# A graph kernel's adjacency: scratch as 512-byte rows, transposed flat in four pieces of 125 columns

## The chip, the cores and the metric

The program runs on one core of a Trainium2 chip. The metric is the device time of one execution in microseconds.

## The reference

A batch of 2048 samples, each with 50 nodes of 32 features, and two maskers. What matters here is how the adjacency is made and used:

```
adj = einsum('bn,tnm->btm', x.reshape(b, 1600), masker_param) + masker_bias
adj = relu(adj).reshape(b, 2, 50, 50)
adj = adj / (adj.sum(axis=-1, keepdims=True) + 1e-6)
m = einsum('btnd,de->btne', h, weight); m = einsum('btnm,btmd->btnd', adj, m)
gates = m @ w_ih.T + b_ih + h @ w_hh.T + b_hh
h = (1 - z) * tanh(r * ng) + z * h        # r, z, ng from gates
```

After that `h` is normalised over the batch and over each sample, scored, and pooled with a softmax. The inputs and outputs are float32; the first stage multiplies in split float32r parts.

## The kernel before, in words

The samples are in 16 tiles of 128. Three stages run one after the other, each with its own block of instructions per engine; semaphores order the engines, and each engine's order is written out by hand.

**First stage** (`stage1`). For each of two blocks of 8 tiles it goes through 10 groups of 500 adjacency columns (`GN` = 10 nodes n by 50 nodes m). A group and a tile make a *window*, 160 in all. PE (`window`, L344) accumulates 38 products of 128x128 by 128x500 into a bank. ACT (`relu`, L227) evacuates it, DVE (`normalise`, L278 to L286) sums the rows and multiplies by the reciprocal, PE (`transposes`, L324) turns the result, ACT (`evacuate`, L233) copies it to `at`, and SP (`store_tile`, L136) stores it to the scratch tensor `adjT` in device memory. PE does the transposes of a window in the middle of the products of the next one, after the fourth pair of chunks (`T_AT`). `u`, `an`, `at` and the banks have two buffers each. DVE writes `an` as 5 pairs of nodes, each node padded from 50 to 64 columns, so that a transpose of 128 columns puts node q on partitions 0 to 49 and node q + 5 on partitions 64 to 113. The pad is zeroed once at the start (L272).

`adjT` is laid out [tile, sample half, m, node, 64 samples]; a row of a store is 5 nodes x 64 samples, 1280 bytes, and there are two stores of 100 rows for each window.

**Second stage** (`stage2`). It works in rounds: 8 rounds of 4 samples per quarter tile make one tile, and two tiles (r = 0, 1, one buffer each) make an iteration. In each round PE aggregates (`aggregate`, L679: the tile's adjacency `adj_sb` times `xs_sb`), ACT and DVE split the result, PE computes the gates (L704, L710), ACT applies the sigmoids and the tanh (L524, L529, L534), DVE updates `h` (L585 to L600). PE turns the chunks of the tile before (L721), ACT copies them to `hC` (L502) and stores them from its own DMA queue (`store`, L509, seven per tile).

SP loads for each tile the adjacency (`load_adj`, L443, one DMA of 100 rows x 25.6 KB into partitions (sample half, m)) and the features `xs_sb` (L445, two DMAs). It issues them for tile t + 2 when PE has aggregated the last round of tile t (`ax_done`); PE waits for them (`adj_loaded`) one round ahead of their first use, at the seventh round of tile t + 1. ACT loads `xg_sb`, the features in another layout, for tile t + 1 in the first round of tile t (`load_xg`, L481), and casts it in four parts (`x_hi`, L490), of which the first stands in the fourth round, in ACT's order ahead of that round's sigmoids. Queue q1 of the profile is SP's, q10 is ACT's.

**Third stage** (`stage3`) reads `h` back (L854, in 512-byte pieces) and pools; it does not touch the adjacency.

Of the kernel before, what the change touches and what calls it, by code (L numbers as in the profile page):

```python
# [15 lines left out]
fp32 = mybir.dt.float32  # L16
# [5 lines left out]
B, N, D, T = 2048, 50, 32, 2  # L22
TN = T * N
P = 128
# [10 lines left out]
GN = 10  # L35
# [3 lines left out]
BLOCKS = TILES // BLK  # L39
ITERS = BLOCKS * GROUPS  # L40
MPAD = 64
SH = P // 2
PAIRS = GN // 2
EPS_ROW = 1e-6
EPS = 1e-5

# [34 lines left out]
def stage1(nc, psum, xT, W, adjT, ident_d):  # L81
    with ExitStack() as ctx:
# [7 lines left out]
        w_raw = sb("w_raw", [P, KC + 1, GW])  # L90
        ident = sb("ident_sb", [P, P])
        u = sb("u", [P, 2, GN, N])
        an = sb("an", [P, 2, PAIRS, 2, MPAD])
        rows = sb("rows", [P, 3, GN])
        at = sb("at", [P, 2, 2, PAIRS, SH])

        x_loaded, ident_loaded = [sem("x_loaded0"), sem("x_loaded1")], sem("ident_loaded")
        w_loaded = [sem(f"w_loaded{i}") for i in range(NU)]
# [2 lines left out]
        mm_done, u_ready, an_ready = sem("mm_done"), sem("u_ready"), sem("an_ready")  # L101
        tr_done, at_ready = sem("tr_done"), sem("at_ready")
        at_stored = [sem("at_stored0"), sem("at_stored1")]
        pad_zeroed, dve_step = sem("pad_zeroed"), sem("dve_step")

        def mm_out(c2):

# [1 line left out]

        def tr_out(c2):  # L110

            return psum[:, (2 + 2 * c2) * BANK:(2 + 2 * c2) * BANK + PAIRS * P]

        block = ctx.enter_context(nc.Block())

        @block.sync
        def _(sp):
            def load_x(bt, half):

                if bt >= 1:  # L120
                    sp.wait_ge(x_ready, 2 * bt - 1 + half)
                k0, k1 = XHALVES[half]
                sp.dma_start(x_raw[:, k0:k1, :], xT[bt, :, k0:k1, :]).then_inc(x_loaded[half], 16)

            def load_w(i, group, after):

                if after is not None:
                    sp.wait_ge(w_ready, after)
                sp.dma_start(w_raw[:, 2 * i:2 * i + 2, :], W[group, i] if isinstance(group, int) else
                             W[bass.ds(group, 1), i].rearrange("g p k n -> p (g k) n")).then_inc(w_loaded[i], 16)  # L130

            def store_tile(c, c2, tile, group):

                sp.wait_ge(at_ready, c + 1)
                for half in range(2):
                    sp.dma_start(adjT[tile, :, :, bass.ds(group * GN + half * PAIRS, PAIRS), :].rearrange("h m c s -> m h c s"),  # L136
                                 at[MPAD * half:MPAD * half + N, c2]).then_inc(at_stored[c2], 16)

            load_x(0, 0)
            for i in range(NU):  # L140
                load_w(i, 0, None)
                if i == 0:
                    load_x(0, 1)
            sp.dma_start(ident[:, :], ident_d).then_inc(ident_loaded, 16)
            for blk in range(BLOCKS):
                for it, group in p1_iters(sp, blk):
                    for w in range(BLK):
                        if isinstance(it, int) and it == 0 and w + 1 < BLK:
                            load_x(w + 1, 0)
                            load_x(w + 1, 1)  # L150
                        if not (isinstance(it, int) and it == ITERS - 1):
                            nxt = 0 if isinstance(it, int) and it % GROUPS == GROUPS - 1 else group + 1

                            for i in range(NU):
                                if w == (min(i + 1, BLK - 2) if isinstance(it, int) and it == 0 else 1):
                                    load_w(i, nxt, it * NU + i + 1)
                        c = it * BLK + w
                        if w > 0:
                            store_tile(c - 1, (w - 1) % 2, blk * BLK + w - 1, group)
                        elif not (isinstance(it, int) and it == 0):  # L160
                            if isinstance(it, int) and it % GROUPS == 0:
                                store_tile(c - 1, 1, blk * BLK - 1, GROUPS - 1)
                            else:
                                store_tile(c - 1, 1, blk * BLK + BLK - 1, group - 1)
                        if isinstance(it, int) and it == GROUPS - 1 and blk + 1 < BLOCKS:
                            load_x(BLK + w, 0)
                            load_x(BLK + w, 1)
            store_tile(ITERS * BLK - 1, 1, TILES - 1, GROUPS - 1)
            sp.wait_ge(at_stored[0], 32 * (ITERS * BLK // 2))
            sp.wait_ge(at_stored[1], 32 * (ITERS * BLK // 2))  # L170

        def split_x_hi(act, bt, half):
            act.wait_ge(x_loaded[half], 16 * (bt + 1))
# [48 lines left out]
        def _(act):  # L222
# [6 lines left out]
            def evacuate(c, c2, start=False):  # L229
                act.wait_ge(tr_done, c + 1)  # L230
                if not start:
                    act.wait_ge(at_stored[c2], 16 * (c - c2))
                nc.scalar.copy(at[:, c2].rearrange("p h q s -> p q h s"),  # L233
                               tr_out(c2).rearrange("p (q h s) -> p q h s", q=PAIRS, h=2)).then_inc(at_ready, 1)

            split_x_hi(act, 0, 0)
            for i in range(NU):
# [31 lines left out]

        @block.vector  # L270
        def _(dve):
            nc.vector.memset(an[:].rearrange("p c q h m -> p (c q h m)"), 0.0).then_inc(pad_zeroed, 1)  # L272
            dve.wait_ge(pad_zeroed, 1)

            def normalise(c, c2, start=False):

                dve.wait_ge(u_ready, c + 1)
# [5 lines left out]
                dve.wait_ge(dve_step, 3 * c + 3)  # L283
                if not start:
                    dve.wait_ge(tr_done, c - 1)
                nc.vector.tensor_tensor(an[:, c2, :, :, 0:N].rearrange("p q h m -> p h q m"),  # L286
                                        u[:, c2].rearrange("p (h q) m -> p h q m", h=2),
                                        rows[:, 2].rearrange("p (h q) -> p h q", h=2).unsqueeze(3).to_broadcast([P, 2, PAIRS, N]),
                                        ALU.mult).then_inc(an_ready, 1)

            split_x_lo(dve, 0, 0)
# [26 lines left out]
        def _(pe):  # L318
            def transposes(c, c2, start=False):
                pe.wait_ge(an_ready, c + 1)  # L320
                if not start:
                    pe.wait_ge(at_ready, c - 1)
                for q in range(PAIRS):
                    last = nc.tensor.transpose(tr_out(c2)[:, q * P:(q + 1) * P],  # L324
                                               an[:, c2, q].rearrange("p h m -> p (h m)"), ident[:, :])
                last.then_inc(tr_done, 1)

            def window(it, w, blk, c, start=False, bank_free=False, none_before=False):
# [54 lines left out]
def stage2(nc, psum, ins, adjT, hF, stats):  # L383


    with ExitStack() as ctx:
# [53 lines left out]
        @block.sync  # L440
        def _(sp):
            def load_adj(tile, r):
                sp.dma_start(adj[:, r], adjT[tile].rearrange("h m c s -> (h m) c s")).then_inc(adj_loaded[r], 16)  # L443
                for half in range(2):
                    sp.dma_start(xs[N * half:N * half + N, r, half], ins["xm"][tile, half]).then_inc(adj_loaded[r], 16)  # L445

# [219 lines left out]
        def _(pe):  # L666
# [15 lines left out]
            def gates(it, s, more):  # L682
# [2 lines left out]
                    pe.wait_ge(xg_ready, (it * 2 + r + 1) * XPARTS)  # L685

                if s == ROUNDS - 2:
                    pe.wait_ge(adj_loaded[1], (it + 1) * 48)
                if s == S - 2 and more:
                    pe.wait_ge(adj_loaded[0], (it + 2) * 48)  # L690
                pe.wait_ge(m_ready, it * S + s + 1)
                xb = [t[:, r, q].unsqueeze(1).to_broadcast([P, T, N * QB]) for t in (xg_hi, xg_lo)]
                def terms(of):
# [34 lines left out]
                        aggregate((s + 1) % S)  # L728
                    gates(it, s, more)

            pe.wait_ge(adj_loaded[0], 48)
            aggregate(0)
            pe.wait_ge(ident_loaded, 16)
            turn(0, True)
# [513 lines left out]


def program(nc, ins, out):  # L1250
    adjT = nc.dram_tensor("adjT", [TILES, 2, N, TN, SH], fp32, kind="Internal").ap()
    hF = nc.dram_tensor("hF", [TILES, P, FC, P], fp32, kind="Internal").ap()
    with nc.psum_tensor("psum", [P, 8 * BANK], fp32) as psum:
        stage1(nc, psum, ins["xT"], ins["W"], adjT, ins["ident"])
# [69 lines left out]
```

## Time and profile before

| | |
|---|---|
| median of 3 runs | 2437.35 us (2435.56 to 2440.09) |
| the profiled execution | 2435.1 us |
| its span | 2433.3 us |
| mean granted TensorE clock | 0.966 |
| PE busy | 2279.1 us, 94% |
| DVE, ACT, POOL busy | 1103.7, 975.1, 135.1 us |

A group of rows in the profile is one line of the kernel on one engine; its busy time is the time in which at least one of its instructions ran, so a mean times a count can be more than the busy time where instructions overlap. A wait is put down to what released it last. A DMA share is the mean over the 16 DMA engines, where packets that overlap on one engine count twice.

### The profile page before, as it was taken

To read this page: it belongs to the slowest core of one execution; us is meant where nothing else is said; L and a number is where in the kernel's file an instruction comes from. 1 tells how busy PE (TensorE), PEld (TensorE's weight loads), DVE (VectorE), ACT (ScalarE), POOL (GpSimd) and SP (SyncE) were. 2 spreads that over 40 slices of the span, in tenths; PEclk is the share of its full clock that TensorE was granted. 3 is DMA by queue.
4 is the path that set the end of the run, shared out by engine and by line. 5 is a ranking of instruction groups with operands and counts; after the bars stand their busy time and mean duration, and the time that the engine had idled before them with its cause. 6 is when DMAs were issued, how large, how long until landed. Compare 5 with 4: busy or idle time off the path is not lost. (4 is left out here: it accounts for less than half of the span.)

```text
span 2433.3 us, 35457 instructions
## 1 busy us (share of the span) xinstructions
PE 2279.1 (94%) x12462; PEld 1815.6 (75%) x12462; DVE 1103.7 (45%) x2191; ACT 975.1 (40%) x1625; POOL 135.1 (6%) x124
## 2 busy tenths in 40 slices
PE   8999999999999999999999993999999999957787
PEld 7888888888888888888888882887878777832333
DVE  5333223233244332223333222677778777764456
ACT  4322212222233222122222121777778777746340
POOL 0000000000000000000000000111111101004230
PEclk9999999999999999999999996999999999977899
DMA  6321122221253220222220213445455454338430
GB/s 225 122 84 48 69 84 88 88 84 39 75 178 119 85 89 28 86 88 85 87 86 28 88 29 107 129 141 149 142 146 153 139 152 135 111 105 204 128 93 5
DMA packets 137744, 250.97 MB, mean 103 GB/s; under 512 B 11734, under 2 KB 97398, under 8 KB 134390
## 3 DMA queue, kind: packets, MB, share of 16 engines
q1 hardware_dynamic: 119546, 212.59, 28.5%
q10 hardware_dynamic: 18144, 37.69, 4.8%
q8 instruction: 29, 0.48, 0.1%
q14 instruction: 25, 0.20, 0.0%
HBM read 182.54 MB, written 67.70 MB: 103 GB/s over the span
## 5 line engine op out<-in xcount | busy, mean ns | idle before, releaser
L344 PE MATMUL psum<-w_hi,x_lo 128*128 128x500 f32 x2080 | 821.0, 395 | 8.2 <-DVE w_lo L214 8.2
L344 PE MATMUL psum<-w_lo,x_hi 128*128 128x500 f32 (+1 forms) x2080 | 810.3, 390 | 0.0
L344 PE MATMUL psum<-w_hi,x_hi 128*128 128x500 f32 x1920 | 746.1, 389 | 0.0
L278 DVE TENSOR_REDUCE rows<-u 128x10 f32<-128x500 f32 x160 | 107.6, 673 | 919.3 <-ACT u L227 919.1
L344 PEld LDWEIGHTS psum<-w_hi,x_lo 128*128 128x128 f32 x2080 | 391.6, 188 | 83.7 <-issue 8.2
L344 PEld LDWEIGHTS psum<-w_lo,x_hi 128*128 128x128 f32 (+1 forms) x2080 | 392.2, 189 | 75.3
L344 PEld LDWEIGHTS psum<-w_hi,x_hi 128*128 128x128 f32 x1920 | 360.9, 188 | 73.4
L233 ACT COPY at<-psum 128x640 f32<-128x640 f32 x160 | 111.0, 693 | 699.8 <-PE psum L324 699.8
L679 PE MATMUL psum<-adj_sb,xs_sb 100*64 100x100 f32 x2048 | 239.7, 391 | 29.6 <-DMA xs_sb<-xm 29.6
L679 PEld LDWEIGHTS psum<-adj_sb,xs_sb 100*64 100x64 f32 x2048 | 197.8, 219 | 64.3 <-issue 64.3
L227 ACT ACTIVATE u<-psum 128x500 f32<-128x500 f32 x160 | 94.0, 587 | 334.2 <-PE psum L344 334.2
L657 POOL TENSOR_TENSOR xg_lo<-xg_sb,xg_hi 128x400 fp32r<-128x400 f32 x64 | 66.8, 1046 | 2044.6 <-ACT xg_hi L490 2044.6
L524 ACT ACTIVATE r_gate<-psum,bias 64x400 f32<-64x400 f32 x256 | 151.0, 590 | 57.0 <-PE psum L704 55.3
L214 DVE TENSOR_TENSOR w_lo<-w_raw,w_hi 128x1000 fp32r<-128x1000 f32 x120 | 144.1, 1201 | 25.8 <-ACT w_hi L208 19.8
L208 ACT CAST w_hi<-w_raw 128x1000 fp32r<-128x1000 f32 (+1 forms) x140 | 135.6, 969 | 46.8 <-PE psum L344 45.3
L529 ACT ACTIVATE psum<-psum,bias 64x400 f32<-64x400 f32 x256 | 141.2, 552 | 3.9 <-DVE hG L600 0.5
L608 DVE BATCH_NORM_STATS2 stats<-hC 128x128 f32 (+1 forms) x400 | 88.5, 281 | 68.9 <-ACT hC L502 68.7
L324 PE MATMUL psum<-ident_sb,an 128*128 128x128 f32 x800 | 113.3, 272 | 3.9 <-DVE an L286 3.9
L324 PEld LDWEIGHTS psum<-ident_sb,an 128*128 128x128 f32 x800 | 97.1, 140 | 24.6 <-DVE an L286 3.0
L286 DVE TENSOR_TENSOR an<-u,rows 128x500 f32<-128x500 f32 x160 | 108.8, 680 | 6.9
L585 DVE SCALAR_TENSOR_TENSOR n_in<-psum,bias,r_gate 128x400 f32<-128x400 f32 x128 | 80.3, 627 | 57.3 <-PE psum L710 28.7
L1027 DVE SCALAR_TENSOR_TENSOR pr<-h,nmu_sb,psum 128x512 f32<-128x512 f32 x100 | 71.1, 743 | 52.2 <-PE psum L1187 31.6
(162 smaller groups left out, 2319.6 us busy)
## 6 DMA issues: line engine op xcount, KB each, us to landing
w_raw<-W SPq DMA_DIRECT2D x140, 500.0 KB, 6.8
adjT<-at SPq DMA_DIRECT2D x320, 125.0 KB
adj_sb<-adjT SPq DMA_DIRECT2D x16, 2500.0 KB
hF<-hC ACTq DMA_DIRECT2D x96, 256.0 KB, 2.2
h<-hF SPq DMA_DIRECT2D x64, 256.0 KB, 4.6
xs_sb<-xm SPq DMA_DIRECT2D x32, 400.0 KB
xg_sb<-xg ACTq DMA_DIRECT2D x14, 800.0 KB, 13.4
h<-hF SPq DMA_DIRECT2D x48, 192.0 KB, 3.8
```

The costliest lines, as they stand in the source:

```text
L208: nc.scalar.copy(w_hi[:, k0:k1, :], w_raw[:, k0:k1, :]).then_inc(w_hi_ready, 1)
L214: nc.vector.tensor_tensor(w_lo[:, k0:k1, :], w_raw[:, k0:k1, :], w_hi[:, k0:k1, :].bitcast(fp32), ALU.subtract).then_inc(w_ready, 1)
L227: nc.scalar.activation(u[:, c2].rearrange("p n m -> p (n m)"), mm_out(c2), ACT.Relu).then_inc(u_ready, 1)
L233: nc.scalar.copy(at[:, c2].rearrange("p h q s -> p q h s"), tr_out(c2).rearrange("p (q h s) -> p q h s", q=PAIRS, h=2)).then_inc(at_ready, 1)
L278: nc.vector.tensor_reduce(rows[:, 0], u[:, c2], AX.X, ALU.add).then_inc(dve_step, 1)
L286: nc.vector.tensor_tensor(an[:, c2, :, :, 0:N].rearrange("p q h m -> p h q m"), u[:, c2].rearrange("p (h q) m -> p h q m", h=2), rows[:, 2 ...
L324: last = nc.tensor.transpose(tr_out(c2)[:, q * P:(q + 1) * P], an[:, c2, q].rearrange("p h m -> p (h m)"), ident[:, :])
L344: last = nc.tensor.matmul(mm_out(w % 2), a[0:r, k, cols], b[0:r, k, :], start=k == 0 and n == 0, stop=k == KF and n == 1)
L524: last = nc.scalar.activation(r_gate[half], rz_bank(pair)[half], ACT.Sigmoid, bias=bias[half, R_G:R_G + 1])
L529: last = nc.scalar.activation(z_bank[half], rz_bank(pair)[other], ACT.Sigmoid, bias=bias[other, Z_G:Z_G + 1])
L608: last = nc.vector.bn_stats(stats[:, bass.ds(tile, 1), c, :].rearrange("p i v -> p (i v)"), hC[:, c, :])
L679: last = nc.tensor.matmul(out_[SH * i:SH * i + SH, :, gi], xs[:, r, :, :, b].rearrange("p h d -> p (h d)"), adj[:, r, :, b], start=True, s ...
```

## The change

The pad goes: DVE writes `an` flat, 500 columns per window, and PE transposes it in four pieces of 125 columns (`RK`, `AK`), so that row p of piece k is adjacency entry 125 k + p. The transposed window then fills 125 partitions x 512 elements, one bank in place of two. ACT copies it as it stands. `adjT` becomes a list of rows [tile, (node, m), 128 samples], 512 bytes each, and one store per window writes 500 of them. The second stage needs (sample half, m) on partitions, so `load_adj` gathers from this list: two DMAs per tile, one per sample half, with 50 partitions and 100 pieces of 64 samples, 256 bytes, on each. The counts of `at_stored` and `adj_loaded` follow.

```diff
@@ -39,8 +39,10 @@
 BLOCKS = TILES // BLK
 ITERS = BLOCKS * GROUPS
 MPAD = 64
+RK = 125
+AK = GW // RK
+assert AK * RK == GW and AK * P == 512
 SH = P // 2
-PAIRS = GN // 2
 EPS_ROW = 1e-6
 EPS = 1e-5
 
@@ -90,9 +92,9 @@
         w_raw = sb("w_raw", [P, KC + 1, GW])
         ident = sb("ident_sb", [P, P])
         u = sb("u", [P, 2, GN, N])
-        an = sb("an", [P, 2, PAIRS, 2, MPAD])
+        an = sb("an", [P, 2, GN, N])
         rows = sb("rows", [P, 3, GN])
-        at = sb("at", [P, 2, 2, PAIRS, SH])
+        at = sb("at", [RK, 2, AK, P])
 
         x_loaded, ident_loaded = [sem("x_loaded0"), sem("x_loaded1")], sem("ident_loaded")
         w_loaded = [sem(f"w_loaded{i}") for i in range(NU)]
@@ -101,7 +103,7 @@
         mm_done, u_ready, an_ready = sem("mm_done"), sem("u_ready"), sem("an_ready")
         tr_done, at_ready = sem("tr_done"), sem("at_ready")
         at_stored = [sem("at_stored0"), sem("at_stored1")]
-        pad_zeroed, dve_step = sem("pad_zeroed"), sem("dve_step")
+        dve_step = sem("dve_step")
 
         def mm_out(c2):
 
@@ -109,7 +111,7 @@
 
         def tr_out(c2):
 
-            return psum[:, (2 + 2 * c2) * BANK:(2 + 2 * c2) * BANK + PAIRS * P]
+            return psum[0:RK, (2 + c2) * BANK:(3 + c2) * BANK]
 
         block = ctx.enter_context(nc.Block())
 
@@ -132,9 +134,8 @@
             def store_tile(c, c2, tile, group):
 
                 sp.wait_ge(at_ready, c + 1)
-                for half in range(2):
-                    sp.dma_start(adjT[tile, :, :, bass.ds(group * GN + half * PAIRS, PAIRS), :].rearrange("h m c s -> m h c s"),
-                                 at[MPAD * half:MPAD * half + N, c2]).then_inc(at_stored[c2], 16)
+                sp.dma_start(adjT[tile, bass.ds(group * GW, GW), :].rearrange("(k p) b -> p k b", p=RK),
+                             at[:, c2]).then_inc(at_stored[c2], 16)
 
             load_x(0, 0)
             for i in range(NU):
@@ -166,8 +167,8 @@
                             load_x(BLK + w, 0)
                             load_x(BLK + w, 1)
             store_tile(ITERS * BLK - 1, 1, TILES - 1, GROUPS - 1)
-            sp.wait_ge(at_stored[0], 32 * (ITERS * BLK // 2))
-            sp.wait_ge(at_stored[1], 32 * (ITERS * BLK // 2))
+            sp.wait_ge(at_stored[0], 16 * (ITERS * BLK // 2))
+            sp.wait_ge(at_stored[1], 16 * (ITERS * BLK // 2))
 
         def split_x_hi(act, bt, half):
             act.wait_ge(x_loaded[half], 16 * (bt + 1))
@@ -229,9 +230,8 @@
             def evacuate(c, c2, start=False):
                 act.wait_ge(tr_done, c + 1)
                 if not start:
-                    act.wait_ge(at_stored[c2], 16 * (c - c2))
-                nc.scalar.copy(at[:, c2].rearrange("p h q s -> p q h s"),
-                               tr_out(c2).rearrange("p (q h s) -> p q h s", q=PAIRS, h=2)).then_inc(at_ready, 1)
+                    act.wait_ge(at_stored[c2], 8 * (c - c2))
+                nc.scalar.copy(at[:, c2].rearrange("p k b -> p (k b)"), tr_out(c2)).then_inc(at_ready, 1)
 
             split_x_hi(act, 0, 0)
             for i in range(NU):
@@ -269,9 +269,6 @@
 
         @block.vector
         def _(dve):
-            nc.vector.memset(an[:].rearrange("p c q h m -> p (c q h m)"), 0.0).then_inc(pad_zeroed, 1)
-            dve.wait_ge(pad_zeroed, 1)
-
             def normalise(c, c2, start=False):
 
                 dve.wait_ge(u_ready, c + 1)
@@ -283,9 +280,7 @@
                 dve.wait_ge(dve_step, 3 * c + 3)
                 if not start:
                     dve.wait_ge(tr_done, c - 1)
-                nc.vector.tensor_tensor(an[:, c2, :, :, 0:N].rearrange("p q h m -> p h q m"),
-                                        u[:, c2].rearrange("p (h q) m -> p h q m", h=2),
-                                        rows[:, 2].rearrange("p (h q) -> p h q", h=2).unsqueeze(3).to_broadcast([P, 2, PAIRS, N]),
+                nc.vector.tensor_tensor(an[:, c2], u[:, c2], rows[:, 2].unsqueeze(2).to_broadcast([P, GN, N]),
                                         ALU.mult).then_inc(an_ready, 1)
 
             split_x_lo(dve, 0, 0)
@@ -320,9 +315,9 @@
                 pe.wait_ge(an_ready, c + 1)
                 if not start:
                     pe.wait_ge(at_ready, c - 1)
-                for q in range(PAIRS):
-                    last = nc.tensor.transpose(tr_out(c2)[:, q * P:(q + 1) * P],
-                                               an[:, c2, q].rearrange("p h m -> p (h m)"), ident[:, :])
+                flat = an[:, c2].rearrange("p n m -> p (n m)")
+                for k in range(AK):
+                    last = nc.tensor.transpose(tr_out(c2)[:, k * P:(k + 1) * P], flat[:, k * RK:(k + 1) * RK], ident[:, :])
                 last.then_inc(tr_done, 1)
 
             def window(it, w, blk, c, start=False, bank_free=False, none_before=False):
@@ -440,7 +435,9 @@
         @block.sync
         def _(sp):
             def load_adj(tile, r):
-                sp.dma_start(adj[:, r], adjT[tile].rearrange("h m c s -> (h m) c s")).then_inc(adj_loaded[r], 16)
+                for half in range(2):
+                    sp.dma_start(adj[N * half:N * half + N, r], adjT[tile, :, SH * half:SH * half + SH].rearrange("(c m) s -> m c s", m=N)
+                                 ).then_inc(adj_loaded[r], 16)
                 for half in range(2):
                     sp.dma_start(xs[N * half:N * half + N, r, half], ins["xm"][tile, half]).then_inc(adj_loaded[r], 16)
 
@@ -685,9 +682,9 @@
                     pe.wait_ge(xg_ready, (it * 2 + r + 1) * XPARTS)
 
                 if s == ROUNDS - 2:
-                    pe.wait_ge(adj_loaded[1], (it + 1) * 48)
+                    pe.wait_ge(adj_loaded[1], (it + 1) * 64)
                 if s == S - 2 and more:
-                    pe.wait_ge(adj_loaded[0], (it + 2) * 48)
+                    pe.wait_ge(adj_loaded[0], (it + 2) * 64)
                 pe.wait_ge(m_ready, it * S + s + 1)
                 xb = [t[:, r, q].unsqueeze(1).to_broadcast([P, T, N * QB]) for t in (xg_hi, xg_lo)]
                 def terms(of):
@@ -728,7 +725,7 @@
                         aggregate((s + 1) % S)
                     gates(it, s, more)
 
-            pe.wait_ge(adj_loaded[0], 48)
+            pe.wait_ge(adj_loaded[0], 64)
             aggregate(0)
             pe.wait_ge(ident_loaded, 16)
             turn(0, True)
@@ -1248,7 +1245,7 @@
 
 
 def program(nc, ins, out):
-    adjT = nc.dram_tensor("adjT", [TILES, 2, N, TN, SH], fp32, kind="Internal").ap()
+    adjT = nc.dram_tensor("adjT", [TILES, TN * N, P], fp32, kind="Internal").ap()
     hF = nc.dram_tensor("hF", [TILES, P, FC, P], fp32, kind="Internal").ap()
     with nc.psum_tensor("psum", [P, 8 * BANK], fp32) as psum:
         stage1(nc, psum, ins["xT"], ins["W"], adjT, ins["ident"])
```

On SP, where the second stage starts (a row names the tile and its source, then the shape as partitions x the rest), the order of the program was:

```order
L448 DMA xg_sb<-xg 128x1600
L443 DMA adj_sb<-adjT 100x6400
L445 DMA xs_sb<-xm 50x2048 x2
L462 DMA ident_sb<-ident 128x128
L448 DMA xg_sb<-xg 128x1600
L443 DMA adj_sb<-adjT 100x6400
L445 DMA xs_sb<-xm 50x2048 x2
```

and is now:

```order
L445 DMA xg_sb<-xg 128x1600
L439 DMA adj_sb<-adjT 50x100x64 x2
L442 DMA xs_sb<-xm 50x2048 x2
L459 DMA ident_sb<-ident 128x128
L445 DMA xg_sb<-xg 128x1600
L439 DMA adj_sb<-adjT 50x100x64 x2
L442 DMA xs_sb<-xm 50x2048 x2
```

The load of the adjacency has become two, each of 50 x 100 pieces of 64 elements, at the same place in SP's queue; nothing else has moved. In the first stage PE's five transposes `128x128 x5` read `125x128 x4` at the same place, and SP's two stores `50x2x320 x2` are one, `125x4x128`.

## Rows read from the trace of the kernel before

**Rows 1.** Busy time by stretches: us, each engine (x instructions), PEclk, DMA share, GB/s.
```profile
100.00:1480.00 1380.00, 1376.17 (x6459) 1146.80 (x6457) 418.20 (x754) 333.70 (x477) 0.00 (x0) 1.00 0.23 79
1480.00:1520.00 40.00, 3.31 (x25) 2.86 (x27) 11.15 (x29) 3.02 (x6) 4.06 (x4) 0.52 0.54 146
1520.00:2110.00 590.00, 568.16 (x4379) 472.00 (x4377) 447.16 (x990) 458.17 (x866) 61.72 (x59) 0.97 0.50 143
```

**Rows 2.** Timeline of PE, end of first stage: start us, us, engine, line, operation.
```profile
1464.97 0.47 PE L344 MATMUL psum<-w_hi,x_lo 128*128 128x500 f32 x1
...
1473.44 0.39 PE L344 MATMUL psum<-w_hi,x_hi 128*128 128x500 f32 x1
1473.66 0.71 PE L324 MATMUL psum<-ident_sb,an 128*128 128x128 f32 x5
1474.13 0.47 PE L344 MATMUL psum<-w_hi,x_lo 128*128 128x500 f32 x1
1474.44 0.39 PE L344 MATMUL psum<-w_lo,x_hi 128*128 128x500 f32 x1
```

**Rows 3.** Waits, whole kernel: total us, times, longest.
```profile
DVE rows L278 <- ACT u L227: 919.1, 135, 7.3
ACT at L233 <- PE psum L324: 699.8, 139, 5.5
...
ACT xg_hi L490 <- DMA xg_sb<-xg: 39.5, 13, 3.9
```

**Rows 4.** Timelines of SP and of PE where the second stage starts.
```profile
1493.54 0.30 SPq L443 DMA_DIRECT2D adj_sb<-adjT  x1
...
1518.19 1.09 PE L679 MATMUL psum<-adj_sb,xs_sb 100*64 100x100 f32 x8 [29.57 <-DMA xs_sb<-xm]
```

**Rows 5.** Stretches between SP's issues of `adj_sb`, second stage, 13 of them.
```profile
1671.63:1710.05 38.42, 37.55 (x300) 31.22 (x299) 30.40 (x69) 30.87 (x59) 4.21 (x4) 1.00 0.52 152
...
1750.95:1791.23 40.28, 38.77 (x301) 32.23 (x301) 31.03 (x71) 31.21 (x60) 4.18 (x4) 0.96 0.50 145
...
sum 520.89, PE 500.69 PEld 416.06 DVE 399.42 ACT 404.31 POOL 54.40; mean PE 38.51 PEld 32.00 DVE 30.72 ACT 31.10 POOL 4.18
```

**Rows 6.** Loads of `xg` (L481) and stores of `hC` (L509): time to landing.
```profile
DMA to landing us min/median/max: 12.4/13.4/14.1
...
DMA to landing us min/median/max: 1.5/2.7/17.1
```

**Rows 7.** Short stretches: `xg` alone, and SP's burst alone.
```profile
1488.00:1490.00 2.00, 0.62 (x2) 0.38 (x2) 2.00 (x1) 0.00 (x0) 0.00 (x0) 0.50 0.89 326
1754.00:1756.00 2.00, 2.00 (x22) 1.74 (x20) 1.33 (x6) 1.85 (x4) 0.00 (x0) 1.00 0.56 128
```

**Rows 8.** DMA queues from 1754 to 1760: packets, MB, share of 16 engines; issues.
```profile
q1 hardware_dynamic: 37, 0.95, 58.7%
...
hF<-hC ACTq DMA_DIRECT2D x1, 256.0 KB, 16.1
```

**Rows 9.** Transposes of the first (L324) and third stage (L1176): ns minimum, median, maximum.
```profile
L324 PE MATMUL psum<-ident_sb,an x800: 271/272/327, 24.8 to 1480.6; 128*128 128x128 f32 x160
...
L1176 PE MATMUL psum<-ident_sb,w x48: 271/273/421, 2243.3 to 2406.6; 128*100 128x128 f32 x48
```

**Rows 10.** A window of the first stage without loads.
```profile
354.00:363.00 9.00, 9.00 (x44) 7.52 (x43) 1.74 (x4) 1.28 (x2) 0.00 (x0) 1.00 0.09 28
```

**Rows 11.** DMA from 2192 to 2222, loads of `h` in 512-byte pieces alone.
```profile
DMA packets 17599, 8.72 MB, mean 291 GB/s; under 512 B 580, under 2 KB 17599, under 8 KB 17599
```

**Rows 12.** SP's waits: end of the first stage.
```profile
SPq L170 <- DMA adjT<-at: 2.1, 1, 2.1
```

**Rows 13.** Timeline of ACT: first cast of `xg` in two tiles.
```profile
1697.40 0.57 ACT L490 CAST xg_hi<-xg_sb 128x400 fp32r<-128x400 f32 x1 [2.29 <-DMA xg_sb<-xg]
...
1777.41 0.55 ACT L490 CAST xg_hi<-xg_sb 128x400 fp32r<-128x400 f32 x1 [2.96 <-DMA xg_sb<-xg]
```

**Rows 14.** SP's issues of the loads of `h`: ns minimum, median, maximum.
```profile
L854 SPq DMA_DIRECT2D h<-hF x112: 367/508/4368, 2180.6 to 2342.7; - x112
```

## The prediction

> **What bounds the kernel now.** I read the busy times by stretches first, then in each stretch what PE waits for, then the DMA queues. By stretches [rows 1] the first stage (up to 1480 us) is PE without a gap at granted clock 1.00, so 2.4 GHz: 1376.17 of 1380 us. Between 1480 and 1520 PE does almost nothing: the second stage waits for its first loads. From 1520 to 2110 PE is busy 96% at mean clock 0.97. The rest is the second stage's tail and the third stage, which the change leaves alone.
>
> In the first stage one window (38 products, one set of transposes) takes 9.16 us: the first product after the transposes starts at 1464.97 in one and at 1474.13 in the next [rows 2]. ACT waits 699.8 us in total for the transposes before its copy, and DVE 919.1 us for ACT [rows 3]. So there only PE counts.
>
> The second stage has two things to see. SP starts its loads at 1493.54, and the first aggregation on PE starts at 1518.19 after 29.57 us idle [rows 4]. Then each tile has a hole: ACT waits for `xg` 13 times, 39.5 us in all [rows 3], about 3.0 us each, just in front of a cast that stands in ACT's order ahead of the sigmoids PE needs. The 13 tile periods that begin and end with SP's `adj_sb` issue sum to 520.89 us, mean 40.07; one of 38.42 has clock 1.00, one of 40.28 has 0.96 [rows 5].
>
> Why is `xg` late? Its load lands a median 13.4 us after its issue [rows 6], while at the start of the stage, with nothing beside it, the same 800 KB moved in some 2 us at 326 GB/s [rows 7]. Stores of `hC` land after 1.5 us at best and 17.1 at worst [rows 6]; one that ACT issued in the middle of SP's burst took 16.1 us [rows 8]. Such a store is 128 rows, 8 for each of 16 DMA engines. From 1754 to 1760 queue q1 moved 37 packets with 0.95 MB, 25.6 KB each, in 58.7% of 16 engines' time: 0.587 x 16 x 6 / 37 = 1.5 us each, up to 2.0 where q1 alone runs (10 engines at 128 GB/s, 12.8 GB/s each) [rows 7, 8]. 8 x 2.0 = 16 us: every row of a store waits behind one 25.6 KB packet of `adj_sb`. The stores, and the `xg` behind them in q10, are held up by the size of the packets, not by the bytes.
>
> **The change, part by part.**
>
> Transposes: 5 become 4 for each of 160 windows. From the last product before them (1473.44) to the second after them (1474.44) is 1.00 us, where two products take 0.45 at their spacing of 0.225 (1473.44 to 1473.66) [rows 2]: 0.55 for five, of which 0.46 (1473.66 to 1474.13) is the five themselves, 0.092 each, and 0.085 a fixed rest. 160 x 0.092 = **-14.7 us**, all on the path. 125 columns in place of 128 in the stationary operand: the third stage's transposes with 100 columns take 273 ns against 272 with 128 [rows 9]; I set it at nothing. ACT's copy of 512 in place of 640 elements, DVE's product into a flat tile, and the memset of `an` that goes lie in idle time of ACT and DVE [rows 3]: nothing.
>
> Stores of the first stage: two DMAs of 100 rows x 1280 B become one of 500 rows x 512 B, with 125 partitions outermost. Quiet windows before show a DMA share of 0.09 at 28 GB/s [rows 10]: 0.09 x 16 x 9 / 200 = 65 ns a row. The nearest row for 512 B is the third stage's load of `h`: 17,599 packets in 30 us on 16 engines, saturated, are 27.3 ns each [rows 11]. If as few as 5 engines carry it, 100 rows each take 2.7 to 6.5 us, inside a window of 9.16 us; the buffer is asked for again two windows on. Hidden. Only the last store shows: SP now waits 2.1 us for it [rows 12]; 2.6 to 7.5 would be its time, +0.5 to +5, I take **+1.5**. The Trainium skill ("DMA: Bandwidth & Descriptors", on why a DMA increments its semaphore by 16) says the engines used are the largest number up to 16 that divides the outermost dimension of both sides: 10 for 100 or 50 partitions, 5 for 125. The trace agrees for the load (q1 alone has a share of 0.56 and 128 GB/s [rows 7], some 9 of 16); for 125 no row shows it. With all 16 engines the sum would be the same, less up to 1 us at the end.
>
> Load of `adj_sb`: one DMA of 100 rows x 25.6 KB becomes two of 5,000 pieces x 256 B, and I take the same 10 engines as now (128 GB/s / 12.8): 1,000 pieces each, for 2.56 MB / 128 GB/s = 20 us now. No row has 256-B pieces in number. From below: a 512-B piece takes 27.3 ns and a 6400-B row of `xg` 6400 B / (326 / 0.89 / 16 = 22.9 GB/s) = 280 ns [rows 7, 11]; a line through both gives 5 + 0.043 x bytes, so 16 ns. From above, if the piece and not the byte costs: 27.3 ns. I take **23 ns**, between, a little nearer to the 512-B row as the closest in size.
>
> The whole burst (adj, two `xs`) and what it holds up run now from 1750.95 [rows 5] to about 1777.4, where `xg` has landed and its cast starts [rows 13], 26.5 us: 20 for adj and 6.5 for the rest. With q10 served sooner I add 2. So a burst after is 1000 t + 8.5 us, t in us a piece: 31.5 at 23 ns, 35.8 at 27.3. It has one tile period to land in, because PE asks for it one tile after the issue.
>
> Start of the second stage: 1000 t in place of 20 us, on the path: **+3** (-4 to +7). SP issues four DMAs in place of three a tile; at 0.29 us and with SP idle between bursts, nothing.
>
> The tile periods: small pieces let q10 in between, so stores and `xg` should land in a few us, and ACT's wait goes. The tile of 38.42 us, at clock 1.00, had a wait of 2.29 [rows 5, 13]: without it 36.1, and with a little given back at the next wait in ACT's order (PE's gates) 36.4. The clock's dips go with the holes. 13 x (40.07 - 36.4) = **-47.7 us** (from below -39.5, the waits alone). What is late next is PE's gate products and ACT's sigmoids, the round's own chain; the burst of 31.5 still fits into 36.4, up to t = 27.9 ns.
>
> Sum against the profiled execution, 2435.1 us: -14.7 + 1.5 + 3 - 47.7 = -57.9, so 2377; the median of the runs is 2.2 above it: **2380 us**. By the bounds: 2371 at 16 ns (start -4, last store +0.5, 47.7 gained), 2395 at 27.3 ns (start +7, last store +5, 39.5 gained).
>
> **Rivals.**
>
> Dear pieces (slower). The kernel asks SP for 10,000 pieces a tile. If a piece of 256 B costs more than one of 512 B, the burst outgrows the tile, PE waits at `adj_loaded`, and the period is the burst. Break-even: 14 (1000 t + 8.5 - 40.07) + (1000 t - 20) + 1.5 = 14.7, t = 31.7 ns, 16% above the 512-B row. At 35 ns: 14 x 3.4 + 15 + 1.5 - 14.7 = +50, 2487. At twice the 512-B price, 54.6: 14 x 23 + 34.6 - 13.2 = +344, 2781. For it: no row bounds it, and the reads jump 25.6 KB at each piece. Against it: the 512-B pieces of `h` jump too and run at 291 GB/s [rows 11]. The same page of the Trainium skill ("Specifications") puts the least size for line rate at 512 B, with a read-modify-write below; it gives no factor, and no run here shows one; taken as two passes it is the 2781.
>
> Blocked queue (slower). If the descriptors of SP's 500-piece-per-engine DMAs must be written before those of ACT's queue come up, stores and `xg` land only at the burst's end: 31.5 us in place of 26.5, the hole grows by 5 us a tile, 13 x 5 = +65; with the transposes, the last store and the start (-14.7 + 1.5 + 3 = -10) 2437 + 65 - 10 = 2492. For: `h` issues take up to 4368 ns on SP when the queue is full [rows 14]. Against: ACT has its own queue.
>
> Holes stay. Engines may change queues only after a group of pieces. With 64 x 23 ns = 1.5 us in a group, 8 turns are 12 us in place of 16, and nearly nothing comes back: 2437 - 10 = 2427. The Trainium skill ("Queues, rings and completion order" on that page) allows up to 64 descriptors in a packet, 9 to 17 typically; by my estimate from 17 and 23 ns, 0.4 us a turn, the hole would be gone. No row shows the grouping.
>
> **How the numbers follow.** A measurement can tell 0.2%, 5 us. Forecast (t up to 28 ns, holes gone): 0.50, range 2368 to 2400. Holes stay: 0.13, mostly faster. Dear pieces: 0.29. Blocked queue: 0.08. Faster 0.60, same 0.04, slower 0.36. The likeliest case gives 2380. The range takes in the forecast, the holes, the blocked queue and dear pieces up to about 38 ns (2437 + 14 x 6.4 + 18 - 13 = 2532); dearer ones, some 0.17, are left out.
>
> **What would show it.** Right: 640 transposes, first-stage window 9.07 us; `xg` landing within 8 us and no ACT wait before L490's cast; tile periods near 36.4 at clock 1.00; q1's share about 10/16 for some 25 us of each tile. Wrong: PE waiting for DMA in front of the aggregation in every tile (dear pieces), `xg` landing with the end of the burst (blocked queue, or groups), or ACT's copy in stage one waiting for a store (5 engines too few).

## The result and the profile after

| | before | after |
|---|---|---|
| median of the runs | 2436.45 us (4 runs) | 2381.14 us (2379.49 to 2383.0, 4 runs) |
| span of the profiled execution | 2433.3 us | 2378.6 us |
| mean granted TensorE clock | 0.966 | 0.971 |

The ratio is 0.9769, with a 95% interval of 0.9753 to 0.9785. The kernel is 55 us faster, and the forecast was 2380 us. The sum is right to about a microsecond, but its terms are not: the largest gain was put too high, and the transposes and the start too low.

The queues of the kernel after, from its page (queue: packets, MB, share of 16 engines' span; below it the issues, with KB and us to landing):

```profile
DMA packets 341903, 250.95 MB, mean 106 GB/s; under 512 B 169494, under 2 KB 303158, under 8 KB 340150
...
q1 hardware_dynamic: 323706, 212.59, 31.6%
q10 hardware_dynamic: 18144, 37.69, 4.8%
...
xg_sb<-xg ACTq DMA_DIRECT2D x14, 800.0 KB, 8.0
...
hF<-hC ACTq DMA_DIRECT2D x16, 64.0 KB, 4.7
```

SP's queue is q1. Its line and that of the small stores read in the kernel before:

```profile
q1 hardware_dynamic: 119546, 212.59, 28.5%
...
hF<-hC ACTq DMA_DIRECT2D x16, 64.0 KB, 16.2
```

So it moves the same 212.59 MB in 323,706 packets, where it had 119,546. Yet `xg` lands after a median 8.0 us (9.9 at most), where it took 13.4 [rows 6].

PE in the first stage, two windows apart by one period (timeline of PE):

```profile
702.88 0.39 PE L339 MATMUL psum<-w_hi,x_hi 128*128 128x500 f32 x1
703.11 0.60 PE L320 MATMUL psum<-ident_sb,an 128*125 128x128 f32 x4
703.47 0.48 PE L339 MATMUL psum<-w_hi,x_lo 128*128 128x500 f32 x1
703.78 0.39 PE L339 MATMUL psum<-w_lo,x_hi 128*128 128x500 f32 x1
...
711.92 0.39 PE L339 MATMUL psum<-w_hi,x_hi 128*128 128x500 f32 x1
712.15 0.60 PE L320 MATMUL psum<-ident_sb,an 128*125 128x128 f32 x4
```

The window is 9.04 us, against 9.16 [rows 2]. Four transposes take 0.60 us where five took 0.71.

The second stage's start (timelines of SP and PE) and SP's last wait of the first stage (SP's waits):

```profile
1476.59 8.12 SPq L439 DMA_DIRECT2D adj_sb<-adjT  x2
...
1500.64 2.70 PE L676 MATMUL psum<-adj_sb,xs_sb 100*64 100x100 f32 x24 [28.88 <-DMA xs_sb<-xm]
```

```profile
SPq L171 <- DMA adjT<-at: 4.1, 1, 4.1
```

From the issue to the first aggregation are 24.05 us, against 24.65 [rows 4]. The last store's wait has grown from 2.1 [rows 12] to 4.1 us.

The tiles of the second stage, by the stretches between SP's issues (two of the 13, and their sum; us, then busy time of PE, PEld, DVE, ACT, POOL, clock, DMA share, GB/s):

```profile
1680.79:1718.30 37.51, 37.51 (x299) 31.20 (x299) 30.88 (x71) 31.16 (x60) 4.17 (x4) 1.00 0.60 156
1718.30:1755.80 37.50, 37.50 (x299) 31.18 (x299) 30.93 (x71) 31.15 (x60) 4.18 (x4) 1.00 0.60 156
...
sum 487.28, PE 487.28 PEld 405.22 DVE 400.40 ACT 404.47 POOL 54.20; mean PE 37.48 PEld 31.17 DVE 30.80 ACT 31.11 POOL 4.17
```

Thirteen tiles take 487.28 us against 520.89 [rows 5]. PE is busy in all of it, at clock 1.00, 2.4 GHz. ACT's waits no longer list one for `xg`; the first cast of a tile stands like this in ACT's timeline, with the `xg` issue 10 us before it:

```profile
1731.48 0.36 ACTq L478 DMA_DIRECT2D xg_sb<-xg  x1
...
1741.32 0.49 ACT L491 CAST m_hi<-psum 128x400 fp32r<-128x400 f32 x1
1741.71 0.53 ACT L487 CAST xg_hi<-xg_sb 128x400 fp32r<-128x400 f32 x1
```

No idle time is marked in front of the cast; before it was 2.29 and 2.96 us in two tiles [rows 13]. This load landed 8.1 us after its issue and the cast starts 10.2 us after it, so 2 us are to spare.

**Where 54.7 us of span went**, by the places of these rows: up to SP's first `adj_sb` issue 1493.54 - 1476.59 = 17.0; from there to the first aggregation 0.6; from the first aggregation to the next issue -0.3 (30.1 before, 30.4 after); 13 tiles 33.6; from the last `adj_sb` issue (2069.19 before, 2018.35 after) to the end 364.1 - 360.3 = 3.9, in which the last of the holes stood:

```profile
2095.79 0.56 ACT L490 CAST xg_hi<-xg_sb 128x400 fp32r<-128x400 f32 x1 [3.03 <-DMA xg_sb<-xg]
```

That cast waited 3.03 us in the kernel before. The sum is 54.8.

### The profile page after: what moved, and what is told of

The parts are those of the page before. It is cut to its first block and busy times, and to the rows that moved or that the text cites. A ratio compares the mean times of both kernels' runs of the same rounds, so it can differ in the third digit from the quotient of the medians.

```text
span 2378.6 us, 34759 instructions
## 1 busy us (share of the span) xinstructions
PE 2250.2 (95%) x12302; PEld 1796.7 (76%) x12302; DVE 1103.6 (46%) x2190; ACT 957.2 (40%) x1625; POOL 134.8 (6%) x124
## 3 DMA queue, kind: packets, MB, share of 16 engines
q1 hardware_dynamic: 323706, 212.59, 31.6%
## 5 line engine op out<-in xcount | busy, mean ns | idle before, releaser
L234 ACT COPY at<-psum 125x512 f32<-125x512 f32 x160 | 93.7, 585 | 677.6 <-PE psum L320 677.6
L320 PEld LDWEIGHTS psum<-ident_sb,an 128*125 128x125 f32 x640 | 94.6, 187 | 17.7 <-DVE an L283 3.0
L320 PE MATMUL psum<-ident_sb,an 128*125 128x128 f32 x640 | 96.5, 273 | 4.0 <-DVE an L283 4.0
```

Source lines behind the costliest of these rows:

```text
L234: nc.scalar.copy(at[:, c2].rearrange("p k b -> p (k b)"), tr_out(c2)).then_inc(at_ready, 1)
L320: last = nc.tensor.transpose(tr_out(c2)[:, k * P:(k + 1) * P], flat[:, k * RK:(k + 1) * RK], ident[:, :])
```

## The experiments

The forecast rested on two separate claims: a transpose left out is worth its time on PE, and the holes of the second stage come from the size of SP's packets. The changed kernel shows both together with a new layout, so each was made alone in the kernel before. Where the number of loads changes, the counts that `adj_loaded` is compared with change too; the diffs leave that out.

**Four transposes, old layout** (`b_four`).

```diff
-                for q in range(PAIRS):
+                for q in range(PAIRS if start else PAIRS - 1):
```

> The kernel before with the fifth of the five transposes of each window left out after the first two windows, so a fifth of the adjacency stored is stale; all else as before. Theory (a transpose costs PE some 0.09 to 0.10 us and nothing hides it): the first stage loses 158 x 0.095 = 15 us, total 2421 us, and the second stage keeps its holes. Rival (the changed kernel's transposes of 125 columns are dearer than those of 128, since their weight load takes 187 in place of 140 ns): the window here comes out clearly under the 9.06 us of the changed kernel, total under 2415 us.

2418.49 us, ratio 0.9935 (0.9913 to 0.9956), 17 us faster. PE's timeline:

```profile
705.06 0.60 PE L324 MATMUL psum<-ident_sb,an 128*128 128x128 f32 x4
...
714.10 0.60 PE L324 MATMUL psum<-ident_sb,an 128*128 128x128 f32 x4
```

The window is 9.04 us, that of the changed kernel, so 125 columns cost nothing against 128 that the window shows, though a weight load of 125 takes 187 ns and one of 128 takes 140. The rival is out. A transpose is worth 9.16 - 9.04 = 0.12 us. The holes stay: ACT waits 38.6 us for `xg`.

**Rows of 6400 B, old layout** (`b_rows6400`).

```diff
-                sp.dma_start(adj[:, r], adjT[tile].rearrange("h m c s -> (h m) c s")).then_inc(adj_loaded[r], 16)
+                for part in range(4):
+                    cs = slice(part * TN // 4, (part + 1) * TN // 4)
+                    sp.dma_start(adj[:, r, cs], adjT[tile, :, :, cs].rearrange("h m c s -> (h m) c s")).then_inc(adj_loaded[r], 16)
```

> The kernel before with the load of the adjacency cut into four DMAs of 25 nodes, rows of 6400 B in place of 25.6 KB; layout, bytes and first stage as before. Theory (each row of ACT's stores and of xg waits behind one packet of SP's queue, so the packet's size makes the hole): xg lands within 9 us, ACT's wait before its cast goes, the tile takes the 37.5 us that PE is busy, total 2436 - 14 x 2.6 = 2400 us. Rival (the hole goes only because 256-byte pieces are gathered in 16 us in place of 20): little changes, 2432 to 2438 us.

2399.14 us, ratio 0.9839 (0.9819 to 0.9859). Its issues of the DMA view, and SP's issues in two neighbouring tiles (timeline of SP):

```profile
xg_sb<-xg ACTq DMA_DIRECT2D x14, 800.0 KB, 9.5
...
hF<-hC ACTq DMA_DIRECT2D x16, 64.0 KB, 8.5
```

```profile
1698.65 1.83 SPq L445 DMA_DIRECT2D adj_sb<-adjT  x4
1736.15 1.93 SPq L445 DMA_DIRECT2D adj_sb<-adjT  x4
```

The tile is 37.50 us, and not one byte has moved elsewhere. Of the 39.5 us that ACT waited for `xg`, 3.4 are left, in three tiles, and they lengthen none: the mean of the 13 is 37.49. The holes went with the rows of 25.6 KB. A store of 64 KB, 8 rows for each engine, landed after a median 16.2 us in the kernel before, 8.5 here, 4.7 in the changed kernel.

**Rows of 12.8 KB** (`b_rows12800`): the same edit with two parts.

> The kernel before with the adjacency's load in two DMAs, rows of 12.8 KB. With 25.6 KB xg lands after 13.4 us and ACT waits 3.0 us a tile, with 6400 B after 9.5 us and no wait. Theory (landing grows with the packet): 10.5 to 11.5 us, a wait of 0 to 1 us that only partly reaches PE, tile 37.5 to 38.3 us, total 2399 to 2410 us. Rival (the number of DMAs or something other than the packet's size helped): as at 6400 B or as at 25.6 KB.

2403.68 us, ratio 0.9878 (0.9852 to 0.9905).

```profile
ACT xg_hi L492 <- DMA xg_sb<-xg: 21.5, 13, 2.5
```

```profile
xg_sb<-xg ACTq DMA_DIRECT2D x14, 800.0 KB, 12.0
...
hF<-hC ACTq DMA_DIRECT2D x16, 64.0 KB, 12.5
```

Landing was 0.5 us over what the expectation allowed, and the wait 1.65 us a tile where 0 to 1 was expected; the time is inside its range. The order is what the theory wants: 25.6, 12.8 and 6.4 KB give a store 16.2, 12.5 and 8.5 us and `xg` 13.4, 12.0 and 9.5 us. And 21.5 us of ACT's wait cost less than the wait: tiles of 37.4 to 39.8 us, mean of the 13 (2041.21 - 1547.81) / 13 = 37.95, 0.45 over PE's 37.50. So of 1.65 us of ACT's wait 1.2 did not reach the period.

The sizes are not what the theory gives. Eight rows that each wait for one packet, at the 12.8 GB/s an engine of [rows 7], would be 16, 8 and 4 us; the store took 16.2, 12.5 and 8.5. The count is right for 25.6 KB alone. Behind shorter rows a store's row waits for more than one of them, and how much goes ahead of it no view shows.

Two other readings fit these three kernels too. The number of loads grows from one to two to four as the rows shrink, and the load gets shorter: by the packets in the traces, a tile's adjacency takes 17.3, 15.9 and 13.9 us from the first packet to the end of the last (means of the 14 tiles after the first two). The changed kernel rules out both. It has two loads, like this one, and they take 20.2 us, yet a store of 64 KB lands after 4.7 us and `xg` after 8.0. With pieces of 128 B (below), four loads and 25.6 us, they land after 4.9 and 6.4 us. The size of the rows is what remains.

**Both** (`b_both`): the two edits above, rows of 6400 B and four transposes.

> The kernel before with both edits: four of five transposes (a fifth of the stored adjacency is stale) and rows of 6400 B. Theory (two gains in different stages, independent): 2436 - 17 - 37 = 2382 us, as the changed kernel, less the 2 us of its longer last store. Rival (they share something): above 2388 us.

2380.15 us, ratio 0.9777 (0.9759 to 0.9795). The two gains add up, and together they are the changed kernel's gain (2381.14 us; the intervals of the two ratios overlap). The new layout in 512-byte rows and 256-byte pieces shows no gain of its own beyond these two. At the start it is even behind: the first aggregation stands at 1497.49 in `b_both` and at 1500.64 in the changed kernel, since SP issues 1.1 us sooner (it waits 2.2 us for the last store in place of 4.1), and from that issue, 1475.48, are 22.0 us in place of 24.05. It is what makes four transposes possible with a full adjacency, and it happens to cut the packets.

**Pieces of 128 B** (`a_p128`), in the changed kernel:

```diff
-                    sp.dma_start(adj[N * half:N * half + N, r], adjT[tile, :, SH * half:SH * half + SH].rearrange("(c m) s -> m c s", m=N)
+                    for a in (0, 32):
+                        sp.dma_start(adj[N * half:N * half + N, r, :, a:a + 32], adjT[tile, :, SH * half + a:SH * half + a + 32].rearrange("(c m) s -> m c s", m=N)
```

> The changed kernel with each gather split again into two DMAs of 32 samples: 20,000 pieces of 128 B for each tile, 2,000 for each of 10 engines, same bytes. If the price is mostly per piece (15 ns as at 256 B): 30 us of pieces, burst some 38 us against a tile of 37.5, start of the second stage 14 us later: 2381 + 14 + 14 x 0.5 to 1 = 2400 us. If the price is mostly per byte (8 to 10 ns): start 2 to 4 us later, tiles unchanged, 2384 us. If pieces below some size cost double (30 ns): burst 68 us, 2381 + 14 x 30 + 45 = 2840 us.

2386.01 us, ratio 0.98 (0.9781 to 0.9819). The tile stays at 37.50 and only the start moves:

```profile
1505.29 3.48 PE L677 MATMUL psum<-adj_sb,xs_sb 100*64 100x100 f32 x32 [33.75 <-DMA xs_sb<-xm]
```

From the issue (1476.42) are 28.87 us, 4.8 more than with 256-B pieces, for 1,000 more pieces on each of 10 engines. The first load alone can be read from the packets of the two kernels, the changed one first (DMA view from 1477 to 1494.4, and from 1477 to 1499.2):

```profile
DMA packets 10039, 2.72 MB, mean 156 GB/s; under 512 B 10020, under 2 KB 10020, under 8 KB 10020
```

```profile
DMA packets 20052, 2.66 MB, mean 120 GB/s; under 512 B 20040, under 2 KB 20040, under 8 KB 20040
```

Its 10,000 pieces move in 16.7 us (1477.5 to 1494.3), and the 20,000 in 21.8. Twice the pieces cost 30% more, so the price goes more by the byte than by the piece. The Trainium skill ("DMA: Bandwidth & Descriptors", "Specifications") sets 512 B as the least size for line rate, with a read-modify-write below. Nothing doubles here at 256 B or at 128 B: in the bare gathers DMA moves 143 to 188 GB/s at 256 B and 107 to 136 at 128 B, in stretches of 2 us:

```profile
1484.00:1486.00 2.00, 0.00 (x0) 0.00 (x0) 0.00 (x0) 0.00 (x0) 1.31 (x2) 0.50 0.82 143
...
1490.00:1492.00 2.00, 0.00 (x0) 0.00 (x0) 0.00 (x0) 0.00 (x0) 0.00 (x0) 0.50 0.80 173
```

```profile
1484.00:1486.00 2.00, 0.00 (x0) 0.00 (x0) 0.00 (x0) 0.00 (x0) 1.13 (x2) 0.50 0.98 107
```

(Busy time by stretches, last three columns clock, DMA share and GB/s: first the changed kernel, then the one with 128 B.)

**Pieces of 64 B** (`a_p64`): the same with `for a in range(0, SH, 16)`.

> The changed kernel with eight gathers a tile, 40,000 pieces of 64 B, 4,000 for each of 10 engines, same bytes. A line through 16 ns at 256 B and 10.4 ns at 128 B gives 7.6 ns at 64 B: 30 us of pieces, burst 38 to 40 us against a tile of 37.5, start 14 us later: 2381 + 14 + 14 x 0 to 3 = 2395 to 2437 us, with PE waiting for xs in every tile if the burst is over 37.5. If the price has a floor of 10 ns a piece: 40 us, burst 48, 2381 + 24 + 14 x 10 = 2550 us.

2500.35 us, ratio 1.0268 (1.0245 to 1.0291), 119 us over the changed kernel. Its waits:

```profile
PE psum L702 <- DMA xs_sb<-xm: 75.5, 14, 12.3
...
PE psum L677 <- DMA xs_sb<-xm: 45.4, 1, 45.4
```

Neither forecast was met: the time lies between 2437 and 2550. This is the slower rival of the prediction, seen at work: PE waits in front of its gates for the loads, in each of 14 tiles. The stretches between SP's issues are (2125.50 - 1552.01) / 13 = 44.1 us. At best the price per piece was near the line (1494 to 1496 moved 91 GB/s, 64 / 9.1 = 7.0 ns for each of 10 engines), but the burst was mis-sized. The 40,000 pieces of the first tile take 33.4 us, 8.4 ns each, where 4,000 x 7.6 ns = 30 was reckoned. In steady tiles, beside ACT's queue, SP's issue of the gathers alone takes 33 to 41 us, and `xs` comes behind it. The start is 16.5 us later (40.55 from issue to first aggregation), and the mean clock over the span is 0.949 in place of 0.971.

**Early gathers** (`a_early`), in the changed kernel:

```diff
+                if first:
+                    sp.wait_ge(zeroed, 1)
                 for half in range(2):
                     sp.dma_start(xs[N * half:N * half + N, r, half], ins["xm"][tile, half]).then_inc(adj_loaded[r], 16)
...
-            sp.wait_ge(zeroed, 1)
-            load_adj(0, 0)
+            load_adj(0, 0, first=True)
```

> The changed kernel with SP's wait for the memset of xs moved behind the two gathers of the first tile, which do not touch xs. Theory (the start of the second stage is the chain memset, gather, xs, and the gather need not wait): first aggregation some 6.4 us earlier, total 2375 us. Rival (the start is held by something else, such as the split weights or xg): no change, 2381 us.

2377.05 us, ratio 0.9759 (0.9737 to 0.9781). The gathers are issued at 1470.20, 6.4 us sooner:

```profile
1495.92 3.47 PE L677 MATMUL psum<-adj_sb,xs_sb 100*64 100x100 f32 x32 [24.19 <-DMA xs_sb<-xm]
```

That is 4.7 us sooner than 1500.64. The missing 1.7 lie at the front of the gathers. From 1471 to 1473 (DMA view) q1 moves 91 packets, and none is a piece:

```profile
DMA packets 91, 0.58 MB, mean 291 GB/s; under 512 B 0, under 2 KB 0, under 8 KB 91
```

They are 6400-byte rows of `xg`, issued just before on the same queue. The first piece moves 3.0 us after the gathers' issue, and 0.95 us after it in the changed kernel, where `xg` was through by then.

**Sixteen engines for the first gathers** (`a_early16`): the first tile's loads each split into partitions 0 to 47 and 48 to 49.

```diff
+                parts = ((0, 48), (48, N)) if first else ((0, N),)
...
+                    for m0, m1 in parts:
+                        then(sp.dma_start(adj[N * half + m0:N * half + m1, r],
+                                          adjT[tile, :, SH * half:SH * half + SH].rearrange("(c m) s -> m c s", m=N)[m0:m1]), m0 == parts[-1][0])
```

> The changed kernel with the early gathers, and the first tile's gathers and xs each split into 48 and 2 partitions. Theory (50 partitions run on 10 DMA engines and 48 on 16, and the gather's time is pieces per engine): 15 us of gather become 9 to 12, first aggregation 3 to 5 us before that of the early version alone, total 2373 us. Rival (the total rate or SP's issuing holds the gather, not the number of engines): no earlier, 2377 us.

2377.82 us, ratio 0.9763 (0.9746 to 0.978): no gain, and the rival holds. The first aggregation starts at 1497.34, 1.4 us later than in the early version. The stretch from 1476 to 1480:

```profile
1476.00:1480.00 4.00, 0.00 (x0) 0.00 (x0) 3.80 (x27) 0.14 (x1) 0.00 (x0) 0.50 1.31 136
```

The share rises to 1.31, so more packets are in flight, but the rate is 136 GB/s, no more than the unsplit gathers of the early version gave (154 and 145 GB/s in the two stretches from 1474 to 1482). The number of engines does not bound these gathers. What does is open: the total rate, or SP, which needs 17.6 us to issue the four gathers where the two took 10.4.

**The pair, side by side** (`a_again`, `a_early_again`).

> The changed kernel once more, beside the early version on the same chip: 2381 us, with a window of 9.04 us, a tile of 37.5 us and the first aggregation 24 us after the gathers' issue, as in its first profile.

> The early version once more, beside the changed kernel on the same chip. Theory (the early gathers bring the first aggregation 4.7 us forward, and nothing later gives it back): 4 to 5 us under the changed kernel. Rival (the 4 us seen across two sets of runs were scatter): within 2 us of it.

The changed kernel 2378.61 us (2377.8 to 2383.05), ratio 0.9761 (0.9744 to 0.9777); the early version 2374.76 us (2371.64 to 2377.93), ratio 0.974 (0.9724 to 0.9755). The medians are 3.9 us apart, as in the first two sets (2381.14 and 2377.05, 4.1 us). The intervals of the ratios still overlap by 0.0011, so the size of the gain is not settled; the direction came twice, and the timelines show 4.7 and 4.5 us at the first aggregation (1495.50 against 1499.97 in this pair). The early version is the fastest kernel of this study, and it leaves nothing out.

## Why the prediction was right, and where its terms were off

**Transposes, -14.7 us.** Right in mechanism, too small. The window lost 0.12 us, not 0.092, so 160 x 0.12 = 19 us. The set itself gave 0.10: from the last product before it to the second behind it are 0.90 us in the changed kernel (702.88 to 703.78) against 1.00. The other 0.02 stand in the products between two sets, 8.14 us (703.78 to 711.92) against 8.16 (1465.28 to 1473.44); why is open. In a small way the row was misread too: 1473.66 to 1474.13 is 0.47, not 0.46. That 125 columns cost nothing holds, shown by `b_four`.

**Last store, +1.5 us.** It is +2.0 (4.1 against 2.1), inside the bounds (2.6 to 7.5 us, which is +0.5 to +5.4). The quiet windows now have a DMA share of 0.11, so 0.11 x 16 x 9 / 500 = 32 ns a row; with 5 engines that is 100 x 32 ns = 3.2 us, with 16 engines 1.0. The growth fits 5 engines, as the Trainium skill's rule in "DMA: Bandwidth & Descriptors" (on why a DMA increments its semaphore by 16) gives for 125 partitions. The trace agrees: while one store moves, and nothing else does, the share is 0.32, some 5 of 16.

```profile
353.00:356.00 3.00, 3.00 (x15) 2.50 (x14) 0.83 (x2) 0.59 (x1) 0.00 (x0) 1.00 0.32 81
```

No copy in the first stage waited for a store.

**Start, +3 us.** It came out at -0.6. Both values of the term failed. One is the 23 ns a piece, "a little nearer to the 512-B row". The lower bound of 16 ns was nearly right: the first tile's 10,000 pieces take 16.7 us, 16.7 ns each on 10 engines. The other is the 20 us for the long rows, worked out from one stretch at 128 GB/s. In the kernel before the first tile's 100 rows move from 1494.4 to 1512.0, 17.6 us. With 16 ns and 20 us the term would have been -4, as far off as the forecast; with both as measured it is -0.9. The line through 512 B and 6400 B (5 ns + 0.043 ns a byte) gave 16 ns at 256 B, and 10.5 at 128 B, where 2,000 pieces on an engine take 21.8 us, 10.9 ns. I had the line and leaned away from it to the nearest row, without a reason in the trace. In the 14 tiles behind the second, beside ACT's queue, the same pieces take 20.2 us on the mean, between the line and the 23.

**Tiles, -47.7 us.** The step that failed is "without it 36.1, and with a little given back 36.4". The tile is 37.50 us, and 13 of them gave 33.6. The error can be read in the very row that was used: the tile of 38.42 us has PE busy for 37.55 [rows 5]. PE could lose only 0.87 us there, though ACT waited 2.29. A wait on ACT was taken off the period as a whole, when what bounds it is PE's own 37.5 us of work. The mean shortfall, 40.07 - 37.50 = 2.57 us a tile, comes from a wait of 3.0 us less the part that hides behind PE, plus the time at a lower clock in some tiles (0.96 in the one of 40.28 us, where PE was busy 38.77 us); how much each gives was not worked out. At 12.8 KB 1.65 us of wait cost only 0.45.

**The mechanism of the holes** was right in that the size of SP's rows makes them. That is shown three ways: rows of 12.8 and of 6.4 KB in the old layout, and the small pieces. That every row of a store waits behind exactly one packet holds for 25.6 KB by the count, and not for shorter rows. "Within 8 us" for the landing of `xg` was nearly met (a median of 8.0, 9.9 at most).

**The rivals.** Dear pieces: not at 256 B, nor at 128 B; at 64 B it came. Its break-even of 31.7 ns was figured against the tile of before, 40.07 us, and the measured price is 16.7 ns in the first load and 20.2 in steady tiles. There the burst is through 26 us after its issue, where 31.5 was reckoned. Blocked queue: out. A store that ACT issued at 1722.43, while SP was still issuing the gathers of 1718.30, took 6.8 us, and the `xg` of 1731.48, issued while their pieces were moving, 8.1. ACT's issues of stores kept to 338 ns, 374 at most. SP's own did not stay at 0.29 us: a gather holds it for 4.0 us (median, 13.9 at most), which cost nothing, since SP has no other work then. Holes stay by groups of pieces: out as a loss, though a 6.8 us landing for 8 rows says that a row still waits; less the 2.0 us of an undisturbed store, some 0.6 us a row, about 30 pieces of 20 ns. That figure is an estimate; the grouping itself is in no view. It would fit the shorter rows as well, behind which a store's row waits for more than one.

So 2380 came partly by luck, from errors that cancel: tiles 14 us too much; transposes, start and the last of the holes (3.9 us after the last issue, in no term) together some 12 us too little. A reader should trust the places and the mechanism, which the experiments carry, and not the agreement of the sum.

## What to carry to other kernels

When a small transfer lands late beside a large one, divide its delay by the rows it has on each DMA engine. If that is the duration of one packet of the large transfer, cut the large one's rows, even if nothing else about it changes; three lines gave 1.6% here. Do not expect half the delay from half the row: it went from 16.2 to 12.5 us. Before a wait on one engine is booked as a gain, look at the busy time of the bounding engine in the same stretch, since the stretch can't go below it. And where two sizes of a transfer give a line, use the line before the nearest row.

## What was not expected of the hardware

- Gathers of 128-B pieces, 20,000 a tile, cost 5 us once and nothing after; of 64 B, 119 us. Between them lies the point where the burst outgrows the tile of 37.5 us.
- The same 2.56 MB, beside the same stores, take 17.3 us in rows of 25.6 KB and 13.9 in rows of 6.4 KB (means of 14 tiles). The cause is open.
- Splitting a gather so that 48 of 50 partitions go apart raised the DMA share from about 0.81 to between 1.20 and 1.32 and lowered the rate from 145 to 154 GB/s to 120 to 141; the cause is open.
- The gathers do not run at one rate, though every piece has 256 B. In the first tile it is 165 GB/s from 1478 to 1480, 143 to 156 up to 1488, then 173 to 188. The cause is open.
- A weight load of 125 columns takes 187 ns and one of 128 takes 140, with no effect on the window.
